# One-hots of a visit's destinations by one DVE comparison in attention and in messages of a graph network

## The chip, the cores and the metric

The kernel runs on one core of a Trainium2 chip as one program. The metric is the device time of that program in microseconds. The engines are TensorE (PE, with its weight loads as PEld), VectorE (DVE), ScalarE (ACT), GpSimd (POOL), and SyncE (SP), which here only starts transfers.

## The reference, cut to what matters

There are 3125 nodes with 64 features and 103125 edges, sorted by destination. Four layers follow each other, each on the normalized x and added to x: a propagation of ten hops, a three-layer graph convolution, attention over each node's incoming edges, and a message layer. The change touches the last two:

```python
# attention
qi = q[tgt]; e = edge_attr @ We; kj = k[src] + e; vj = v[src] + e
alpha = jnp.sum(qi * kj, axis=-1) / math.sqrt(C)         # two heads of 64
amax = jax.ops.segment_max(alpha, tgt, num_segments=n)
ex = jnp.exp(alpha - amax[tgt])
den = jax.ops.segment_sum(ex, tgt, num_segments=n)
agg = jax.ops.segment_sum((ex / (den[tgt] + 1e-08))[:, :, None] * vj, tgt, num_segments=n)
# messages
msg = jax.nn.relu(jnp.concatenate([edge_feat, hid[src]], axis=1) @ W1 + b1)
msg_sum = jax.ops.segment_sum(msg, dst, num_segments=N_NODES)
```

## The kernel before

The edges are cut into 403 tiles of 256, two halves of 128 edges on the partitions, and the nodes into blocks of 64 destinations. Since the edges are sorted, a tile meets one block or a few; a pair of a tile and a block that it may meet is a visit, and there are 451 visits (V2). The last 48 visits of a stage need no new tile. Which block and tile belong to a visit is found on the chip: each engine that needs the numbers loads them once in eight visits (`Blocks`) and addresses its operands through registers.

`stage_tables` makes, among others, `rel2`: for each edge of each visit its destination minus 64 times the block, in 32 bit floats. A value from 0 to 63 is a destination inside the block, anything else means that the edge belongs to another visit. Its steps on DVE are a chain: each waits for the one before. `iotaH` holds 0, 1, 2, ... in 16 bits on every partition.

`stage_attend` (from L1390 on). POOL gathers the source rows of each tile by two indirect DMAs of 128 rows (L1451), up to eight tiles ahead; SP brings edge features and the block's transformed queries (L1437, L1442). PE runs a loop with one step per visit: it transposes the next tile (L1465), scores a visit in one of two banks, transposes the exponentials of the visit two before (L1484) and sums the one three before (L1492). The score is the one-hot times `pen` (L1473) plus the query product (L1476). The one-hot of DVE holds 0 at an edge's destination and -1 elsewhere, in both heads' 64 columns, and `pen` is the unit matrix times 1e30, so that destinations that are not the edge's own get -1e30. DVE does for a visit: the maximum over a row (L1541), a one-hot half for the visit two ahead (L1531), the new running maximum (L1547), the other half (L1531), the difference (L1552), the accumulation of the visit three before (L1558) and the store of the maximum (L1561). ACT copies the transposed tile (L1503) and exponentials (L1508), and takes the two exponentials (L1513, L1514).

`stage_messages` (from L1800 on). Of each eight tiles, POOL gathers six from the message table (L1870), and DVE adds the gathered rows to the product of the edge features (L1902) in a bank (L2000). For the other two PE looks the rows up itself: DVE makes 25 comparisons of 512 edges with a chunk of the table (L2006), PE multiplies each with the table (L1909). ACT applies relu (L1945 from memory, L1942 from the bank). The one-hot of a visit is made by ACT in three instructions, max(0, 1 - |rel2 - iota|): twice the absolute value (L1951) and once the rest (L1957). PE sums the visit by the one-hot two steps later (L1918, four banks), and DVE accumulates (L2012). The one-hots are 32 bit floats there, in four buffers.

`stage_build` already makes its one-hots by paired comparisons (L447 to L449), with both operands read as pairs of 16 bit numbers.

Of the kernel before, what the change touches and what calls it, by code (L numbers as in the profile page):

```python
# [7 lines left out]
F32 = mybir.dt.float32  # L8
F16 = mybir.dt.float16
# [3 lines left out]
ALU = mybir.AluOpType  # L13
ACT = mybir.ActivationFunctionType
# [3 lines left out]
P = 128  # L18
# [11 lines left out]
T1 = -(-EDGES // TE)  # L30
# [26 lines left out]
BD = 64  # L57
# [3 lines left out]
V2 = T1 + J2 - 1  # L61
V2P = 460
# [40 lines left out]
class Mem:  # L103


    def __init__(self, nc, ctx):
        sb = lambda name, shape, dt: ctx.enter_context(nc.sbuf_tensor(name, shape, dt))
# [6 lines left out]
        self.work2 = sb("work2", [P, NDST + NCH * D], F32)  # L114
        self.rel2 = sb("rel2", [P, 2, V2P], F32)
        self.src2 = sb("src2", [P, 2, V2P], I32)
# [12 lines left out]
        sem = lambda n: ctx.enter_context(nc.semaphore(n))  # L129
# [31 lines left out]
    def small(self, i):  # L161

        return self.smalls[:, i * D:(i + 1) * D]

    def zbuf(self, k):

        base = self.work[:, 0:NCH * D] if k == 0 else self.work2[:, 3 * DC:3 * DC + NCH * D]
        return base.bitcast(F16).rearrange("p (a s d) -> p a s d", a=NCH, s=2)
# [5 lines left out]
def stage_tables(nc, m, last0, last, dst, src, edges):  # L174
# [4 lines left out]
    with ExitStack() as ctx:  # L179
        sem = lambda n: ctx.enter_context(nc.semaphore(n))  # L180
# [3 lines left out]
        def take(n):  # L184
            at[0] += n
            return raw[:, at[0] - n:at[0]]
# [19 lines left out]
        jI = m.work2[:, 2 * V0P:3 * V0P].bitcast(I32)  # L206
        src2F = take(2 * V2P).rearrange("p (h v) -> p h v", h=2)
        wmax, wall = take(1), take(1)
# [10 lines left out]
        for arr in range(4):  # L219
            for k in range(0, K1, 4):  # L220
                n = min(4, K1 - k)
                groups.append(([f1[:, k + i, arr, :] for i in range(n)], tabT[:, arr, k * P:(k + n) * P]))
        for arr, to in enumerate((m.rel2, src2F)):
            for h in range(2):
                groups.append(([f2[:, k, arr, h * P:(h + 1) * P] for k in range(K2)], to[:, h, 0:V2P]))
# [66 lines left out]
        def _(dve):  # L292
            chain = m.dve_step.on(dve)
# [5 lines left out]
            for s in schemes:  # L299
# [4 lines left out]
                for c in range(s["C"]):  # L304
                    ins = dve.tensor_scalar(s["cmp"][:, c, :], iotaF[:, 0:s["VP"]], s["end"][:, c:c + 1], None, ALU.is_gt)
                ins.then_inc(s_cmp, 1)
            for c in range(C0):
                ins = dve.tensor_scalar(cmpJ[:, c, :], iotaF[:, 0:J0], schemes[0]["blkF"][:, c:c + 1], None, ALU.is_ge)
# [71 lines left out]
            j2 = schemes[1]["jv"][:, 1:V2P + 1]  # L380
            for h in range(2):
                chain(dve.scalar_tensor_tensor(m.rel2[:, h, :], j2, -float(BD), m.rel2[:, h, :], ALU.mult, ALU.add))
            chain(dve.tensor_copy(m.src2[:, :, :], src2F))
# [819 lines left out]
BIG = 1e30  # L1203
# [37 lines left out]
def wait(eng, sem, n):  # L1241

    if not isinstance(n, int) or n > 0:
        eng.wait_ge(sem, n)
# [145 lines left out]
def stage_attend(nc, m, keep, x_out, q_out, ea, x_t, q_t):  # L1390
# [4 lines left out]
    with ExitStack() as ctx:  # L1395
# [121 lines left out]
        def _(dve):  # L1517
            dve.memset(rows[:, :, :, ONE:ONE + 1], 1.0)
            dve.memset(nmax, LOW)
            dve.tensor_scalar(pen, m.ident[:, :], BIG, None, ALU.mult)  # L1520
            for hd in range(HEADS):
# [4 lines left out]

            def onehot(v, s):

                if s == 0:
                    wait(dve, scored, v - 3)  # L1530
                ins = dve.tensor_scalar(oh[v % 4][:, s, :], iota2, m.rel2[:, s, v:v + 1], -1.0, ALU.is_equal, ALU.add)  # L1531
                if s == 1:
                    ins.then_inc(oh_ready, 1)

            for i in range(-2, V2 + 3):
# [7 lines left out]
                if v < V2:  # L1543
                    onehot(v, 0)
                if inside:
                    dve.wait_ge(s_small, 3 * i + 1)
                    dve.tensor_tensor(nm[s3], nmj, rm[s3], ALU.min).then_inc(s_small, 1)  # L1547
                if v < V2:
                    onehot(v, 1)
                if inside:  # L1550
# [249 lines left out]
def stage_messages(nc, m, keep, w1, w_out, b_out, o_in, ef_t, src, g_t):  # L1800

    with ExitStack() as ctx:
# [11 lines left out]
        oh = [halves(take(2 * BD)) for _ in range(4)]  # L1814
        away = [halves(take(2 * BD)) for _ in range(2)]
        T = [halves(take(2 * D)) for _ in range(4)]
# [16 lines left out]
        oh_ready = sem("ms_oh")  # L1833
        away_ready = sem("ms_away")
        summed = sem("ms_A")
# [87 lines left out]
        def _(act):  # L1923
            act.wait_ge(init, 1)
            for i in range(-2, V2):
                t = i
# [10 lines left out]
                if 0 <= t < T1:  # L1937
# [8 lines left out]
                    ins.then_inc(m_ready, 1)  # L1946
                v = i + 1
                if 0 <= v < V2:
                    wait(act, oh_ready, v - 1)
                    for s in range(2):  # L1950
                        ins = nc.scalar.activation(away[v % 2][:, s, :], m.iotaH[:, 0:BD], ACT.Abs, bias=m.rel2[:, s, v:v + 1], scale=-1.0)  # L1951
                    ins.then_inc(away_ready, 1)
                v = i
                if 0 <= v < V2:
                    act.wait_ge(away_ready, v + 1)
                    wait(act, summed, v - 3)
                    nc.scalar.activation(oh[v % 4], away[v % 2], ACT.Relu, bias=1.0, scale=-1.0).then_inc(oh_ready, 1)  # L1957

        @block.vector
        def _(dve):  # L1960
# [13 lines left out]
            def split():  # L1974
# [13 lines left out]
                dve.tensor_tensor(table[:, :, 1, :], wide, table[:, :, 0, :], ALU.subtract).then_inc(s_max, 1)  # L1988

            for i in range(-1, V2 + 3):  # L1990
                if i == 3:
                    split()
                t = i
                if 0 <= t < T1 and not on_pe(t):
# [180 lines left out]
```

## Time and profile before

| what | value |
|---|---|
| median of 3 runs | 3705.48 us |
| lowest and highest | 3702.94, 3708.67 us |
| span of the profiled execution | 4103.0 us |
| profiled execution's own time | not listed beside the runs; its span stands for it |
| busy share PE, PEld, DVE, ACT, POOL | 77%, 48%, 48%, 39%, 40% |
| TensorE clock granted, mean | 0.832 |
| attention's visits | 1640 to 2995 us |
| messages' visits | 3064 to 4070 us |

The profiled execution is 397.5 us longer than the median of the runs without a profile. Its durations are those of single instructions, start to end; instructions of one engine overlap by some tens of nanoseconds, so starts are compared with starts where pace matters. Register instructions don't count as busy.

### The profile page before, as it was taken

The page shows a single profiled execution, that of the slowest core. Times are in us where ns is not written, and L with a number is a line of the kernel's source. Part 1 is how long each engine was busy: PE and PEld are TensorE (multiplying, and loading weights), DVE is VectorE, ACT ScalarE, POOL GpSimd, SP SyncE. Part 2 cuts the span into 40 slices and gives each one's busy share as a digit, 9 for nine tenths or more (in the row PEclk, how much of TensorE's full clock was granted, in tenths as well). Part 3 has the DMA queues.
Part 4 walks back from the last instruction along what each step waited for, and adds up shares of the span by engine and source line. Part 5 has one row for each costly group of instructions (what it writes and reads, how often), then busy time and mean ns, then how long its engine had stood idle before and what let it go on. Part 6 is the DMA issues. An engine that isn't in the chain of part 4 may idle for free. (4 is left out here: it accounts for less than half of the span.)

```text
span 4103.0 us, 80080 instructions
## 1 busy us (share of the span) xinstructions
PE 3139.2 (77%) x17480; PEld 1972.5 (48%) x17480; DVE 1986.4 (48%) x6935; ACT 1606.3 (39%) x4621; POOL 1627.3 (40%) x1766
## 2 busy tenths in 40 slices
PE   3788788879997797577777777777866778787877
PEld 2444444444443343455566656556643444444445
DVE  6656666556656115344444444444673444444442
ACT  1555555413322001233333333333453444444445
POOL 2000000024333001666666666666106666666660
PEclk7899898999998998687777777877977888888885
DMA  1111111125557995322222222222112222222220
GB/s 38 57 59 57 57 59 59 51 93 193 188 177 261 406 360 185 65 54 55 54 55 54 55 54 53 54 55 54 40 28 56 66 63 66 64 66 63 66 61 13
DMA packets 417722, 370.64 MB, mean 90 GB/s; under 512 B 175608, under 2 KB 342232, under 8 KB 417336
## 3 DMA queue, kind: packets, MB, share of 16 engines
q1 hardware_dynamic: 365912, 315.65, 23.8%
q0 software_dynamic: 46144, 48.98, 6.5%
q8 instruction: 198, 3.24, 0.3%
q10 hardware_dynamic: 5280, 1.23, 0.1%
q14 instruction: 188, 1.54, 0.1%
HBM read 279.65 MB, written 86.00 MB: 89 GB/s over the span
## 5 line engine op out<-in xcount | busy, mean ns | idle before, releaser
L1451 POOL DMA_INDIRECT big<-row_table,src x806 | 761.5, 945 | 487.3 <-issue 183.4
L1870 POOL DMA_INDIRECT big<-message_table,src x610 | 612.0, 1003 | 394.5 <-DVE big L2000 172.1
L1476 PE MATMUL banks<-big 97*128 x902 | 399.8, 534 | 148.6 <-issue 138.1
L1492 PE MATMUL banks<-big 128*128 x1804 | 349.0, 326 | 174.8 <-ACT big L1508 110.1
L486 PE MATMUL banks<-work 128*128 128x226 f16 x1197 | 350.3, 293 | 138.6 <-issue 131.0
L1492 PEld LDWEIGHTS banks<-big 128*128 128x128 f32 x1804 | 312.4, 244 | 202.5 <-issue 202.1
L1909 PE MATMUL banks<-big 128*128 128x512 f16 x1225 | 395.6, 441 | 4.4 <-DVE big L1988 4.4
L850 PE MATMUL banks<-big,work 128*128 128x512 f16 (+1 forms) x1750 | 352.1, 359 | 22.3 <-DVE work L984 17.4
L1541 DVE TENSOR_REDUCE big<-banks 128x1 f32<-128x256 f32 x451 | 189.4, 420 | 332.5 <-PE banks L1476 183.8
L1508 ACT COPY big<-banks 128x256 f32<-128x256 f32 x451 | 169.8, 377 | 439.5 <-remote 194.0
L1918 PEld LDWEIGHTS banks<-big 128*64 128x64 f32 x1804 | 173.8, 164 | 343.6 <-issue 343.0
L1918 PE MATMUL banks<-big 128*64 x1804 | 247.5, 268 | 116.5 <-issue 98.3
L487 PE MATMUL banks<-work 128*128 128x200 f16 x1197 | 335.6, 280 | 0.0
L488 PE MATMUL banks<-work 128*128 128x200 f16 x1197 | 326.9, 273 | 0.0
L429 POOL COPY work<-work 128x100 f16<-128x100 f16 x120 | 35.9, 300 | 666.9 <-DVE work L452 649.9
L1558 DVE SCALAR_TENSOR_TENSOR big<-big,banks 128x97 f32 x451 | 142.4, 316 | 325.0 <-remote 208.5
L486 PEld LDWEIGHTS banks<-work 128*128 128x128 f16 x1197 | 121.9, 102 | 363.1 <-issue 350.1
L512 ACT ACTIVATE work<-banks 128x800 f32<-128x800 f32 x196 | 164.3, 838 | 330.6 <-PE banks L488 330.6
L908 POOL TENSOR_TENSOR work<-work 128x400 f16<-128x400 f32 x196 | 180.1, 946 | 284.8 <-DVE work L977 244.2
L2006 DVE TENSOR_SCALAR big<-big 128x512 f16<-128x512 f16 x1225 | 281.6, 285 | 2.3
L2000 DVE TENSOR_TENSOR big<-banks,big 128x128 f32<-128x128 f32 x305 | 87.3, 286 | 399.8 <-remote 257.3
L1476 PEld LDWEIGHTS banks<-big 97*128 97x128 f32 x902 | 177.4, 244 | 198.9 <-issue 196.4
(338 smaller groups left out, 5835.8 us busy)
## 6 DMA issues: line engine op xcount, KB each, us to landing
big<-weights_halves SPq DMA_DIRECT2D x16, 6400.0 KB, 20.8
weights_dense<-work SPq DMA_DIRECT2D x196, 200.0 KB, 1.9
work<-weights_dense SPq DMA_DIRECT2D x196, 200.0 KB, 2.7
weights_halves<-work SPq DMA_DIRECT2D x98, 400.0 KB, 2.6
big<-q_table SPq DMA_DIRECT2D x451, 64.0 KB
big<-in_ef SPq DMA_DIRECT2D x403, 64.0 KB
big<-in_ea SPq DMA_DIRECT2D x403, 32.0 KB
big<-row_table,src POOLq DMA_INDIRECT x806
```

The source lines that it names most:

```text
L486: pe.matmul(to(CW, CW + CAW), rows[:, 0, t, :], cols[:, t, :], start=False, stop=True, skip_group_check=True)
L487: pe.matmul(to(0, CW), rows[:, 1, t, :], cols[:, t, 0:CW], start=False, stop=True, skip_group_check=True)
L488: pe.matmul(to(0, CW), rows[:, 2, t, :], cols[:, t, 0:CW], start=False, stop=True, skip_group_check=True).then_inc(vis_done, 1)
L850: ins = pe.matmul(m.PB[c % 4][:, 0:width(c)], z[k][:, a, :, :], counts[:, a, c * DC:c * DC + width(c)], start=(a == 0), stop=(a == NCH - 1))
L1451: po.indirect_dma_start(rows[:, t % RT, s, 0:D], None, x_t.rearrange("a p c -> (a p) c"), bass.IndirectOffsetOnAxis(ap=m.src2[:, s, t:t + ...
L1476: pe.matmul(psS[v % 2], qT[v % R][0:XW, :], XF[0:XW, bass.ds(slot, 1), :].rearrange("p t e -> p (t e)"), start=False, stop=True).then_inc( ...
L1492: ins = pe.matmul(psA[v % 2], PT[v % 2][:, s * P:(s + 1) * P], rows[:, bass.ds(slot, 1), s, :].rearrange("p t c -> p (t c)"), start=(s == ...
L1541: dve.tensor_reduce(rm[s3], psS[i % 2], op=ALU.max, axis=X, negate=True).then_inc(s_small, 1)
L1870: po.indirect_dma_start(G[n % R][:, s, :], None, g_t.rearrange("a p c -> (a p) c"), bass.IndirectOffsetOnAxis(ap=m.src2[:, s, t:t + 1], ax ...
L1909: pe.matmul(psH[q % 2], table[:, a, :, :].rearrange("p s d -> p (s d)"), hot[n % HOT], start=(a == 0), stop=(a == NCH - 1)).then_inc(hot_u ...
L1918: ins = pe.matmul(psA[v % 4], oh[v % 4][:, s, :], M[:, bass.ds(slot, 1), s, :].rearrange("p t c -> p (t c)"), start=(s == 0), stop=(s == 1))
L2006: dve.tensor_scalar(hot[n % HOT], key[q % 2], float(P * a - CENTER), None, ALU.is_equal).then_inc(hot_ready, 1)
```

## The change

`rel2` becomes a table of 16 bit floats in which every number stands twice. It is clamped to -1 to 64 first, since large differences would not be exact in 16 bits. In attention one DVE instruction compares both halves of the tile with `iota2`; it gives 1 where the destination is another one and 0 where it is the edge's own, and `pen` changes its sign. It stands where the first of the two stood. In messages the three ACT instructions, their buffers and their semaphore are gone, and one DVE comparison stands at the head of each step of DVE's loop.

```diff
-        self.rel2 = sb("rel2", [P, 2, V2P], F32)
+        self.rel2 = sb("rel2", [P, 2, V2P, 2], F16)
+    def places(self, v, n):
+        return self.rel2[:, :, v, :].unsqueeze(2).to_broadcast([P, 2, n // 2, 2])
...
-                chain(dve.scalar_tensor_tensor(m.rel2[:, h, :], j2, -float(BD), m.rel2[:, h, :], ALU.mult, ALU.add))
+                chain(dve.scalar_tensor_tensor(dst2F[:, h, :], j2, -float(BD), dst2F[:, h, :], ALU.mult, ALU.add))
+                chain(dve.tensor_scalar(dst2F[:, h, :], dst2F[:, h, :], -1.0, float(BD), ALU.max, ALU.min))
+                chain(dve.tensor_copy(m.rel2[:, h, :, :], dst2F[:, h, :].unsqueeze(2).to_broadcast([P, V2P, 2])))
...
-            dve.tensor_scalar(pen, m.ident[:, :], BIG, None, ALU.mult)
+            dve.tensor_scalar(pen, m.ident[:, :], -BIG, None, ALU.mult)
...
-            def onehot(v, s):
-                if s == 0:
-                    wait(dve, scored, v - 3)
-                ins = dve.tensor_scalar(oh[v % 4][:, s, :], iota2, m.rel2[:, s, v:v + 1], -1.0, ALU.is_equal, ALU.add)
-                if s == 1:
-                    ins.then_inc(oh_ready, 1)
+            both = iota2.rearrange("p (r u) -> p r u", u=2).unsqueeze(1).to_broadcast([P, 2, P // 2, 2])
+            def others(v):
+                wait(dve, scored, v - 3)
+                dve.tensor_tensor(oh[v % 4].rearrange("p s (r u) -> p s r u", u=2), both, m.places(v, P), ALU.not_equal).then_inc(oh_ready, 1)
...
                 if v < V2:
-                    onehot(v, 0)
+                    others(v)
                 if inside:
                     dve.wait_ge(s_small, 3 * i + 1)
                     dve.tensor_tensor(nm[s3], nmj, rm[s3], ALU.min).then_inc(s_small, 1)
-                if v < V2:
-                    onehot(v, 1)
...
-                v = i + 1
-                if 0 <= v < V2:
-                    wait(act, oh_ready, v - 1)
-                    for s in range(2):
-                        ins = nc.scalar.activation(away[v % 2][:, s, :], m.iotaH[:, 0:BD], ACT.Abs, bias=m.rel2[:, s, v:v + 1], scale=-1.0)
-                    ins.then_inc(away_ready, 1)
-                v = i
-                if 0 <= v < V2:
-                    act.wait_ge(away_ready, v + 1)
-                    wait(act, summed, v - 3)
-                    nc.scalar.activation(oh[v % 4], away[v % 2], ACT.Relu, bias=1.0, scale=-1.0).then_inc(oh_ready, 1)
...
+            here = m.iotaH[:, 0:BD].rearrange("p (r u) -> p r u", u=2).unsqueeze(1).to_broadcast([P, 2, BD // 2, 2])
             for i in range(-1, V2 + 3):
                 if i == 3:
                     split()
+                v = i
+                if 0 <= v < V2:
+                    wait(dve, summed, v - 3)
+                    dve.tensor_tensor(oh[v % 4].rearrange("p s (r u) -> p s r u", u=2), here, m.places(v, BD), ALU.is_equal).then_inc(oh_ready, 1)
```

## Rows read from the trace of the kernel before

**Rows 1.** Busy us by stretch: PE, PEld, DVE, ACT, POOL; clock, DMA share, GB/s

```profile
1640.00:2890.00 1250.00, 903.02 (x4730) 731.22 (x4726) 532.21 (x2763) 463.87 (x1576) 762.21 (x807) 0.77 0.27 55
2890.00:2995.00 105.00, 85.34 (x573) 68.91 (x573) 75.60 (x397) 53.87 (x179) 0.00 (x0) 0.98 0.12 34
3064.00:4007.00 943.00, 729.57 (x3775) 396.87 (x3776) 397.63 (x1930) 431.35 (x1675) 612.04 (x610) 0.82 0.28 64
4007.00:4070.00 63.00, 43.77 (x263) 31.60 (x262) 15.03 (x69) 48.16 (x179) 0.00 (x0) 0.58 0.01 3
```

**Rows 2.** The page: gathers, busy us, mean ns of one, idle before

```profile
L1451 POOL DMA_INDIRECT big<-row_table,src x806 | 761.5, 945 | 487.3 <-issue 183.4
L1870 POOL DMA_INDIRECT big<-message_table,src x610 | 612.0, 1003 | 394.5 <-DVE big L2000 172.1
```

**Rows 3.** Timeline of a stall: start us, us, [idle before <-releaser]

```profile
2398.15 0.95 POOL L1451 DMA_INDIRECT big<-row_table,src  x1 [0.30 <-issue]
...
2398.38 0.39 PE L1465 MATMUL banks<-ident,big 128*97 128x128 f32 x2
...
2400.50 0.32 DVE L1558 SCALAR_TENSOR_TENSOR big<-big,banks 128x97 f32 x1 [3.31 <-remote]
2400.67 0.94 POOL L1451 DMA_INDIRECT big<-row_table,src  x1 [1.57 <-remote]
```

**Rows 4.** Waits of the whole run: engine, line, releaser: us, times, longest

```profile
DVE big L2000 <- remote: 257.3, 63, 15.3
...
DVE big L1558 <- remote: 208.5, 122, 3.3
...
PE banks L1902 <- ACT big L1942: 35.2, 23, 2.6
...
PE banks L1473 <- DVE big L1531: 3.7, 8, 0.5
```

**Rows 5.** Groups by shape on DVE, whole run

```profile
L2012 DVE TENSOR_TENSOR big<-big,banks 64x65 f32 x451 | 94.5, 210 | 189.6 <-PE banks L1918 105.1 <-issue 41.2 <-remote 37.3
L2000 DVE TENSOR_TENSOR big<-banks,big 128x128 f32<-128x128 f32 x305 | 87.3, 286 | 399.8 <-remote 257.3 <-PE banks L1902 122.2 <-issue 19.3
...
L449 DVE TENSOR_TENSOR work<-iotaH,work 128x260 f16<-128x260 f16 x120 | 34.4, 287 | 0.0
...
L383 DVE CAST src<-big 128x920 int32<-128x920 f32 x1 | 0.6, 639 | 0.0
```

**Rows 6.** Timeline of DVE in one visit of attention

```profile
2394.53 0.41 DVE L1541 TENSOR_REDUCE big<-banks 128x1 f32<-128x256 f32 x1
2394.86 0.25 DVE L1531 TENSOR_SCALAR big<-big,rel 128x128 bf16<-128x128 f16 x1
2395.23 0.16 DVE L1547 TENSOR_TENSOR big<-big 128x1 f32<-128x1 f32 x1
...
2395.47 0.15 DVE L1552 TENSOR_TENSOR big<-big 128x1 f32<-128x1 f32 x1
```

**Rows 7.** Timeline of messages behind its last gather

```profile
4028.35 1.47 PE L1918 MATMUL banks<-big 128*64 x8 [0.16 <-issue]
...
4028.97 0.22 DVE L2012 TENSOR_TENSOR big<-big,banks 64x65 f32 x1 [0.36 <-DVE big L2012]
...
4030.30 0.59 ACT L1951 ACTIVATE big<-iotaH,rel 128x64 f32<-128x64 f16 x2
...
4030.86 0.69 PE L1918 MATMUL banks<-big 128*64 x4 [0.16 <-issue]
...
4031.14 0.58 ACT L1951 ACTIVATE big<-iotaH,rel 128x64 f32<-128x64 f16 x2
...
4033.86 0.69 PE L1918 MATMUL banks<-big 128*64 x4 [1.30 <-DVE big L2012]
```

**Rows 8.** Timeline of messages, table comparisons beside a gather

```profile
3605.97 0.69 DVE L2006 TENSOR_SCALAR big<-big 128x512 f16<-128x512 f16 x3
...
3606.41 1.20 POOL L1870 DMA_INDIRECT big<-message_table,src  x1 [0.30 <-issue]
```

More of the change, by code:

```diff
@@ L206, in stage_tables @@
         jI = m.work2[:, 2 * V0P:3 * V0P].bitcast(I32)
-        src2F = take(2 * V2P).rearrange("p (h v) -> p h v", h=2)
+        src2F, dst2F = (take(2 * V2P).rearrange("p (h v) -> p h v", h=2) for _ in range(2))
         wmax, wall = take(1), take(1)
@@ L222, in stage_tables @@
                 groups.append(([f1[:, k + i, arr, :] for i in range(n)], tabT[:, arr, k * P:(k + n) * P]))
-        for arr, to in enumerate((m.rel2, src2F)):
+        for arr, to in enumerate((dst2F, src2F)):
             for h in range(2):
@@ L1814, in stage_messages @@
         oh = [halves(take(2 * BD)) for _ in range(4)]
-        away = [halves(take(2 * BD)) for _ in range(2)]
         T = [halves(take(2 * D)) for _ in range(4)]
@@ L1833, in stage_messages @@
         oh_ready = sem("ms_oh")
-        away_ready = sem("ms_away")
         summed = sem("ms_A")
@@ L1924, in _ @@
             act.wait_ge(init, 1)
-            for i in range(-2, V2):
+            for i in range(-2, T1):
                 t = i
```

## The prediction

> **What bounds the kernel now.** I read the page first, for the shares: TensorE (PE) is busy 77% of the span, DVE 48%, ACT 39%, POOL 40%, and none of these says what a visit waits for. So I cut the span at the stages that the change touches [rows 1]. Attention takes 1640 to 2995 us, the last 105 us of it without any gather; messages takes 3064 to 4070, the last 63 us nearly all without. In the two stretches with gathers PE is busy 72% and 77%, DVE 43% and 42%, ACT 37% and 46%, POOL 61% and 65%. TensorE's granted clock is 0.77 and 0.82 there, a mixture of its two levels, 1.2 and 2.4 GHz. No engine is full, and the share of POOL hides something: a gather is busy 0.945 us [rows 2], but 0.30 us of issue stands before each even when nothing else does [rows 3]. So 806 gathers need 806 x 1.25 = 1007 us of the 1250 us, and in messages, where one takes 1.003 us, 610 x 1.308 = 798 us of the 943 us. The loops run 243 and 145 us over POOL's floor.
>
> What fills the difference? The waits answer with a releaser that the profile can't name: "remote" stands behind 209 us of waiting of the accumulation in attention (L1558) and 257 us of the add in messages (L2000) [rows 4]. The timeline of one such stall shows what it is: the K transposes start at 2398.38 and take 0.39 us, yet DVE and POOL, which wait for PE's work, both resume only at 2400.50 and 2400.67, after 3.31 and 1.57 us of idleness [rows 3]. All the news of PE is late at once. I found such stalls only where gathers run.
>
> The profiled execution spans 4103.0 us, and the median of the runs is 3705.5, which is 397.5 less. The excess over POOL's floor is 243 + 145 = 388 us. I take these for the same time: without the profiler the two loops run close to POOL's gather rate. That is an inference, not a reading, and the chances below allow for its being wrong. The sum is made as differences on the profiled execution and carried over in microseconds.
>
> **Part 1, the tables.** rel2 is now made by a sum into a scratch row, a clamp and a doubling copy, for each of two halves. The sum stays. The copy writes 920 elements a partition, 0.64 us by L383; the clamp has half as many, and I give it the same for an upper bound [rows 5]. This is a serial chain on DVE with nothing beside it: 2 x 2 x 0.64 = +2.6 us, and not below +1.3.
>
> **Part 2, attention.** For each of 451 visits two comparisons of 0.25 us (L1531) go [rows 6], and one of 128 x 256 elements, all 16 bit, comes. L449 is nearly this instruction (a paired comparison with iotaH, 260 elements): 287 ns [rows 5]. DVE's busy time falls by 451 x (0.50 - 0.287) = 96 us. Little of it lies on a path, and the order of starts shows why [rows 6]. The first comparison starts 0.33 us after the reduction, and the minimum L1547 starts 0.37 us after that, although the comparison took only 0.25: register instructions for the block's column stand between (they don't count as busy). A comparison of 0.287 fits into the same 0.37. The second comparison runs inside the wait from L1547 to L1552: 0.24 us apart, of which L1547 itself is 0.16. Taking it out can bring L1552 forward by 0.08 at most; since L1552 must still see L1547's semaphore, I take half, 0.04. PE scores with two banks, so the loop from score through exponential to score spans two visits, and a visit gets 0.02 of it. If this loop set every visit, that were 403 x 0.02 = 8 us in the stretch with gathers; since POOL's floor sets part of them I take 4, and for the 48 visits behind them 1. The ends: 0, and 451 x 0.08 = 36 us. The one-hot is also ready earlier, but PE's wait for it is 3.7 us in all [rows 4]. The pen only changes its sign, and PE's work not at all.
>
> **Part 3, messages.** ACT loses two instructions and one (L1951 twice, L1957) a visit; its pace with them, in the stretch without gathers, is 0.84 us a visit (4030.30 to 4031.14) [rows 7]. DVE gets one comparison of 128 x 128 elements with 16 bit inputs and a 32 bit result. The trace has none. From below: 210 ns, L2012 with 65 elements. From above: 286 ns, L2000, 128 elements in 32 bit [rows 5]. I take 286, the row with the same element count. That is 451 x 0.286 = 129 us more on DVE, which brings it from 398 of 943 us in the gather stretch to about 515, 55%. The new wait (for the sum of visit v-4) adds nothing: DVE has waited for the same sum one step earlier, to accumulate it. Behind the new instruction on DVE queue the add L2000 of the tile, which frees POOL's buffer (eight tiles deep) and PE's bank (two deep), then the table comparisons and the accumulation. PE needs the one-hot of visit v two steps later, so none of this is tight.
>
> In the gather stretch I cost all this at 0: the cover is POOL, 6 tiles of 8 gathered, 12 x 1.308 = 15.7 us for eight visits. DVE needs in the same eight visits, from start to start, 25 x 0.23 for the table comparisons (0.69 for three [rows 8]), 6 x 0.29 for the adds, 8 x 0.58 for the accumulations (0.22 and 0.36 before it [rows 7]) and 8 x 0.29 for the new one: 14.4 us. That is under 15.7, but not by much. If the cover is gone, the relief of ACT counts too: PE waits 35.2 us for L1942, ACT's exit of the bank [rows 4], which no longer stands behind one-hots.
>
> In the 48 visits behind the last tile ACT's pace is close to what is seen. PE takes 0.69 + 0.16 = 0.85 us a visit there, and 1.47/2 = 0.735 where two visits run together; every eighth visit waits 1.3 us more for DVE, which loads its next block numbers [rows 7]. Without ACT's pace I give PE 0.735 for each visit: 48 x 0.115 = 6 us less. The ends: 0, because DVE must then do 0.58 for the accumulation and part of 0.29 for the comparison (0.87 at worst, no better than now), and 12, if the wait of each eighth visit shrinks too.
>
> **The sum.** +2.6 - 4 - 1 - 6 = -8.4 us, so 3705.5 - 8.4 = 3697 us, 0.2% faster. What a measurement of this kernel can tell from no change is 0.2%, 7.4 us: the forecast lies on that border.
>
> **A rule to weigh.** In attention two one-hot comparisons fall beside many a gather, and the gathers take 945 ns on average, with 0.94 in the rows that I looked at [rows 2, 3]: at most 0.005 x 806 = 4 us hang on it. In messages a gather beside trains of table comparisons takes 1.20 us [rows 8], and the mean is 1.003. The Trainium skill, page "SBUF — State Buffer", section "Who interferes with whom", says that a tensor_scalar can take the port pair that DVE shares with GpSimd and then holds off descriptor writing, while a tensor_tensor with two SBUF inputs contends only with GpSimd's reads. By that rule the change helps attention's gathers and leaves those of messages alone. The trace agrees for the trains in messages and shows next to nothing of it in attention.
>
> **The rivals.**
> 1. The forecast, small gains at the ends of the two loops: 0.47; 3688 to 3706.
> 2. The loops are not at POOL's floor without the profiler, and latency counts. Then attention's 451 x 0.04 = 18, the 6 of messages' end and 0 to 35 for PE's wait on L1942 come off, and the tables' 2.6 come on: 3684 to 3649, at half the wait 3667. For it: PE also waits in the gather-free stretches. Against it: 388 against 397. Chance 0.18.
> 3. Nothing moves: DVE's comparison takes the place of ACT's pace at the end of messages, and attention hides all: 3705.5 + 2.6 = 3708. Chance 0.14.
> 4. Slower: the new comparison slows POOL's gathers, which are the floor. The trains cost (1003 - 945) x 610 = 35 us over 1225 table comparisons, 0.029 us each; 451 more at this price are 13 us, at twice the price, as they lengthen a train, 26. Without gains and with the tables that gives 3721 to 3734; if each held a gather up for its full 0.286 wherever one runs (65% of the time), 84 us. It decides from 0.035 us for each, where it has eaten the 8.4 us and added 7.4. Against it: attention's L1547 and L1552, which have two inputs in SBUF too, though of one column, run beside its gathers, and these take 945 ns. Chance 0.13.
> 5. Slower: DVE's 14.4 us for eight visits is too low and passes POOL's 15.7, and the adds come late. At 1.5 to 1.8 us more for eight visits it costs 49 x 0.2 to 0.5 = 10 to 25 us: 3715 to 3730. Chance 0.08.
>
> **How the numbers follow.** Case 1 gives 0.26 to faster and 0.21 to no change, case 2 goes to faster, 3 to no change, 4 and 5 to slower: 0.44, 0.35, 0.21. The range runs from the middle of case 2, rounded to 3670, into case 4, 3722, and leaves out about half of either.
>
> **What would show it.** Right: in attention L1547's counterpart still starts 0.37 us after the comparison, L1552's about 0.20 after L1547's; a visit of messages behind the last tile takes about 0.9 us, waits for block numbers included, and not 0.85 + 1.3/8 = 1.01; gathers keep 945 and 1003 ns; PE no longer waits for L1942. Wrong: gathers in messages above 1.03 us (case 4); the new comparisons far from 0.29 us; DVE above 60% in messages with PE waiting for L2000 (case 5); or loops that get shorter by tens of microseconds with POOL's times unchanged, which would say that POOL's floor was not the bound.

## The result and the profile after

The changed kernel takes 3750.97 us (median of 4 runs, 3747.97 to 3754.76), the kernel before 3706.15 us (4 runs, 3702.94 to 3708.67). The ratio is 1.0117, with a 95% interval from 1.0104 to 1.0131: 44.8 us or 1.2% slower. The forecast was 3697 us with a range up to 3722; sign and range are both wrong.

The page of the changed kernel, busy shares and the two gathers:

```profile
span 3752.9 us, 78285 instructions
...
PE 2949.0 (79%) x17480; PEld 1839.4 (49%) x17480; DVE 2101.8 (56%) x6939; ACT 1319.1 (35%) x3268; POOL 1669.7 (44%) x1766
...
L1457 POOL DMA_INDIRECT big<-row_table,src x806 | 764.1, 948 | 249.7 <-issue 228.8
L1871 POOL DMA_INDIRECT big<-message_table,src x610 | 651.5, 1068 | 251.4 <-issue 177.8
```

Attention's gathers keep their length (945 ns before, [rows 2]). Those of messages go from 1003 to 1068 ns: 610 gathers, 651.5 us busy and not 612.0. Of the 251.4 us of idle time in front of them 177.8 is issue, and 65.7 stands before the first one, so in the loop POOL waits for next to nothing.

Busy time by stretch of the changed kernel: attention with gathers and behind them, messages with gathers and behind them (us, then PE, PEld, DVE, ACT, POOL, granted clock, DMA share, GB/s).

```profile
1650.00:2666.00 1016.00, 799.98 (x4804) 641.63 (x4800) 537.85 (x2411) 484.76 (x1605) 765.87 (x807) 0.90 0.33 69
2666.00:2760.00 94.00, 77.58 (x516) 62.31 (x516) 65.74 (x302) 46.65 (x152) 0.00 (x0) 0.98 0.12 32
2829.00:3667.00 838.00, 659.22 (x3836) 364.97 (x3837) 509.98 (x2347) 178.73 (x500) 651.52 (x610) 0.93 0.30 72
3667.00:3720.00 53.00, 34.71 (x202) 25.45 (x202) 21.54 (x103) 0.31 (x1) 0.00 (x0) 0.50 0.01 2
```

These can't be set against [rows 1] directly: the span is 350 us shorter than the 4103.0 us of the first profile of the kernel before, although the kernel is slower. So the first experiment was the kernel before once more.

### The profile page after: what moved, and what is told of

It reads as the page before. It is cut to its first block and busy times, and to the rows that moved or that the text cites. A ratio compares the mean times of both kernels' runs of the same rounds, so it can differ in the third digit from the quotient of the medians.

```text
span 3752.9 us, 78285 instructions
## 1 busy us (share of the span) xinstructions
PE 2949.0 (79%) x17480; PEld 1839.4 (49%) x17480; DVE 2101.8 (56%) x6939; ACT 1319.1 (35%) x3268; POOL 1669.7 (44%) x1766
## 5 line engine op out<-in xcount | busy, mean ns | idle before, releaser
L1871 POOL DMA_INDIRECT big<-message_table,src x610 | 651.5, 1068 | 251.4 <-issue 177.8
L1482 PE MATMUL banks<-big 97*128 x902 | 347.5, 471 | 88.7 <-issue 84.4
L1910 PE MATMUL banks<-big 128*128 128x512 f16 x1225 | 349.7, 398 | 4.7 <-DVE big L1977 4.7
L1946 ACT ACTIVATE big<-big 128x128 f32<-128x128 f32 x305 | 94.9, 311 | 644.7 <-DVE big L1994 631.2
L2000 DVE TENSOR_SCALAR big<-big 128x512 f16<-128x512 f16 x1225 | 308.6, 306 | 0.0
L1498 PE MATMUL banks<-big 128*128 x1804 | 289.6, 287 | 0.0
L1919 PE MATMUL banks<-big 128*64 x1804 | 225.1, 253 | 56.7 <-issue 39.8
L1471 PE MATMUL banks<-ident,big 128*97 128x128 f32 x806 | 189.2, 320 | 102.3 <-DMA big<-row_table,src 90.7
L1065 PE MATMUL banks<-big,work 128*128 128x512 f16 x900 | 217.7, 406 | 60.8 <-DMA big<-weights_halves 51.2
L1498 PEld LDWEIGHTS banks<-big 128*128 128x128 f32 x1804 | 264.2, 211 | 0.4 <-issue 0.3
```

Source lines behind the costliest of these rows:

```text
L1065: pe.matmul(out, z[l % 2][:, a, :, :], st[buffer(l, c)][:, 0:n // BP, s, a * BP:(a + 1) * BP], start=(a == 0 and s == 0), stop=False)
L1482: pe.matmul(psS[v % 2], qT[v % R][0:XW, :], XF[0:XW, bass.ds(slot, 1), :].rearrange("p t e -> p (t e)"), start=False, stop=True).then_inc( ...
L1498: ins = pe.matmul(psA[v % 2], PT[v % 2][:, s * P:(s + 1) * P], rows[:, bass.ds(slot, 1), s, :].rearrange("p t c -> p (t c)"), start=(s == ...
L1871: po.indirect_dma_start(G[n % R][:, s, :], None, g_t.rearrange("a p c -> (a p) c"), bass.IndirectOffsetOnAxis(ap=m.src2[:, s, t:t + 1], ax ...
L1910: pe.matmul(psH[q % 2], table[:, a, :, :].rearrange("p s d -> p (s d)"), hot[n % HOT], start=(a == 0), stop=(a == NCH - 1)).then_inc(hot_u ...
L1919: ins = pe.matmul(psA[v % 4], oh[v % 4][:, s, :], M[:, bass.ds(slot, 1), s, :].rearrange("p t c -> p (t c)"), start=(s == 0), stop=(s == 1))
```

## The experiments

Each ratio is against the kernel before on the same chip, in the same series of runs.

**The kernel before once more** (no edit).

> The kernel before, unchanged, for a second profile. Theory A (the kernel runs at POOL's gather rate, and the stalls of the first profile belonged to that execution): a span near 3705 us, attention's gathers start every 1.25 us in the mean, messages' gathers every 1.30 to 1.31 us (mean duration 1.00 us), against 1.373 (1.068 us) in the kernel after; about 38 us of the difference of 45 us lie there. Theory B (latency of ACT and DVE bounds the loops, and POOL only seems to): POOL waits for other engines in both loops as in the first profile, and the mean distance of gathers is clearly above 1.31 us in messages.

It took 3707.0 us with a span of 3705.2 us. Its page and its stretch of messages with gathers:

```profile
L1451 POOL DMA_INDIRECT big<-row_table,src x806 | 761.8, 945 | 248.9 <-issue 226.5
L1870 POOL DMA_INDIRECT big<-message_table,src x610 | 610.1, 1000 | 250.6 <-issue 177.1
```

```profile
2822.00:3618.00 796.00, 638.78 (x3830) 357.21 (x3830) 433.58 (x1944) 439.15 (x1706) 610.05 (x610) 0.95 0.31 76
3618.00:3673.00 55.00, 36.36 (x209) 26.30 (x208) 12.49 (x56) 40.43 (x149) 0.00 (x0) 0.50 0.01 2
```

A profile without stalls exists: neither loop has a wait for "remote" in it (the two of the whole run, 4.1 us, belong to the stages ahead), and its span with 1.8 us around it is the run's own time. The loops run at POOL's rate: from the first to the last gather start, attention takes 1006.3 us (1.250 a gather), messages 794.8 us (1.305), the 1007 and 798 us that the prediction had worked out.

With this trace the account of one profiled execution of each kernel can be made. The starts of the first and the last gather of each loop in the changed kernel:

```profile
1655.80 1.19 POOL L1457 DMA_INDIRECT big<-row_table,src  x1 [4.08 <-POOLq L1264]
...
2664.58 0.95 POOL L1457 DMA_INDIRECT big<-row_table,src  x1 [0.30 <-issue]
...
2829.09 0.96 POOL L1871 DMA_INDIRECT big<-message_table,src  x1 [65.72 <-POOLq L1570]
...
3665.39 0.95 POOL L1871 DMA_INDIRECT big<-message_table,src  x1 [0.31 <-issue]
```

| stretch | before | changed | difference |
|---|---|---|---|
| start to first gather of attention | 1650.1 | 1655.8 | +5.7 |
| attention's gathers | 1006.3 | 1008.8 | +2.5 |
| last one to messages' first gather | 165.8 | 164.5 | -1.3 |
| messages' gathers | 794.8 | 836.3 | +41.5 |
| last gather to the end of the span | 88.3 | 87.5 | -0.8 |

The sum, 47.6 us, is the difference of the spans (47.7). Of the +5.7 the tables are 2.2; the rest is what single executions differ by in the stages ahead, which the change doesn't touch: an execution of the changed kernel further down has its first gather at 1648.3 us and 1006.5 us of attention's gathers. Only the +41.5 stands out of this.

**Each half of the change alone.** The rival theories were now: A, the comparison in messages lengthens the gathers; C, the tables and attention have a part in it. Attention alone (the doubled numbers are copied at the stage's start from `rel2`, which stays a table of 32 bit floats; messages as before):

```diff
-                ins = dve.tensor_scalar(oh[v % 4][:, s, :], iota2, m.rel2[:, s, v:v + 1], -1.0, ALU.is_equal, ALU.add)
+                dve.tensor_tensor(oh[v % 4]..., both, rel16[:, :, v, :]..., ALU.not_equal).then_inc(oh_ready, 1)
```

> Only attention gets the single paired comparison; its 16 bit pairs are copied from the unchanged 32 bit rel2 when the stage begins (about 2 us), and messages keeps ACT's three instructions. Theory A (POOL's gathers set attention, and nearly all of the loss is in messages, where the change of that stage alone gave 1.010): ratio 1.000 to 1.002, attention's gathers every 1.25 us, messages' every 1.305. Rival C (attention lost too, by a comparison with two inputs in SBUF beside the gathers): 1.003 or more, most of it in longer gathers.

Measured: 3705.5 us against 3709.5, ratio 0.9994 [0.9985, 1.0004]; gathers 946 and 1003 ns, attention's first to last start 1006.7 us. Attention's half does nothing that can be told from the scatter.

Messages alone (attention as before, the same copy at the head of messages):

```diff
-                        ins = nc.scalar.activation(away[v % 2][:, s, :], m.iotaH[:, 0:BD], ACT.Abs, ...)
-                    nc.scalar.activation(oh[v % 4], away[v % 2], ACT.Relu, ...)
+                    dve.tensor_tensor(oh[v % 4]..., here, rel16[:, :, v, :]..., ALU.is_equal).then_inc(oh_ready, 1)
```

> Only messages gets DVE's comparison, from pairs copied when the stage begins; attention keeps two comparisons. Theory A (the whole loss is that messages' gathers take longer beside a DVE that has no pause left): ratio 1.011 to 1.013, gathers of messages 1.06 to 1.08 us in the mean. Rival C (the loss is spread over both stages or sits in the tables): 1.004 to 1.008.

Measured: 3743.2 us, ratio 1.0102 [1.0084, 1.0120]; gathers 945 and 1067 ns. The loss is this half; the ratio is just under the expected 1.011 to 1.013, the gathers are inside the expected length.

**Is it the instruction on DVE, or that ACT no longer makes the one-hots?** Two kernels keep ACT's one-hots and add to DVE, where the comparison would stand, an instruction whose result nobody reads (both also make the copy at the head of messages). The expectations speak of two theories: P, that an instruction of DVE holds a gather up by its second input in SBUF; D, that any further instruction does it, because it closes DVE's pauses. The first kernel adds the comparison itself.

```diff
+                    dve.tensor_tensor(nowhere[v % 2]..., here, rel16[:, :, v, :]..., ALU.is_equal).then_inc(idle_done, 1)
```

> The kernel before, ACT's one-hots kept, plus the comparison of the kernel after at the same place, its result thrown away. Both theories P and D: gathers of messages 1.36 to 1.38 us apart, ratio 1.010 to 1.012. A rival E, that the kernel after lost by taking the one-hots from ACT (their order or their time of arrival) and not by DVE's instruction, expects 1.000 here.

Measured: 3741.4 us, ratio 1.0093 [1.0076, 1.0110]; gathers of messages 1061 ns, 1.366 us apart. What was taken from ACT has next to no part in the loss, and saves nothing.

The second is a reduction over 128 numbers of `iotaH`, with one input and one number a partition as output.

```diff
+                    dve.tensor_reduce(nowhere[v % 2][:, 0, 0:1], m.iotaH[:, 0:P], op=ALU.max, axis=X).then_inc(idle_done, 1)
```

> The kernel before, ACT's one-hots kept, plus one reduction of 128 columns of iotaH to one column on DVE at the head of each visit of messages (0.25 to 0.3 us, one input, result thrown away). Theory P (a gather is held up by DVE instructions that use a second SBUF port or input): the reduction doesn't count, messages' gathers stay at 1.305 us apart and the ratio at 1.000 to 1.001. Theory D (any further instruction on DVE closes the pauses in which a gather gets through): gathers at 1.36 to 1.38 us apart, ratio 1.010.

Measured: 3738.9 us, ratio 1.0083 [1.0067, 1.0100]; gathers of messages 1052 ns, 1.357 us apart: a little under what theory D expected, and far from theory P. So neither the second input nor the size of the output makes up most of the cost; the same 0.27 us on DVE costs nearly the same.

**The comparison with its iota in PSUM.** Bank 5 holds the iota as 32 bit floats, so only three banks are left for the sums.

```diff
-        psA = [m.PB[2 + i][0:BD, 0:MW] for i in range(4)]
+        psA = [m.PB[2 + i][0:BD, 0:MW] for i in range(3)]
+            dve.tensor_copy(m.PB[5][:, 0:BD], m.iotaH[:, 0:BD])
-            here = m.iotaH[:, 0:BD]...
+            here = m.PB[5][:, 0:BD]...
```

> The kernel after, with messages' comparison reading iota from a PSUM bank of its own as 32 bit numbers, so that it has one input in SBUF; the sums get three banks instead of four. The comparison should take about 0.29 us as now. Theory P: gathers of messages return to 1.30 us apart or less, and the ratio to the kernel before is 0.998 to 1.002. Theory D: nothing changes, 1.011 to 1.013.

Measured: 3726.7 us, ratio 1.0046 [1.0029, 1.0063]; gathers of messages 1019 ns. The instruction is no shorter (0.27 us), and the loss is less than half. Both expectations missed: P expected no loss, D all of it.

Now one gather in each of four traces, beside the same work of DVE: the turn of eight tiles in which PE looks up two tiles itself, so that DVE has no landing to wait for and runs without a stop. In the changed kernel the lines of messages on DVE are others: L2000 is the table comparison (L2006 before), L2006 the accumulation (L2012 before), L1994 the add (L2000 before), L1986 the new comparison. First the kernel before (start us, us, engine, line):

```profile
3299.05 0.68 DVE L2006 TENSOR_SCALAR big<-big 128x512 f16<-128x512 f16 x3
...
3299.19 1.46 POOL L1870 DMA_INDIRECT big<-message_table,src  x1 [0.30 <-issue]
...
3299.65 0.20 DVE L2012 TENSOR_TENSOR big<-big,banks 64x65 f32 x1
3299.78 0.68 DVE L2006 TENSOR_SCALAR big<-big 128x512 f16<-128x512 f16 x3
...
3300.39 0.20 DVE L2012 TENSOR_TENSOR big<-big,banks 64x65 f32 x1
3300.90 0.29 DVE L2000 TENSOR_TENSOR big<-banks,big 128x128 f32<-128x128 f32 x1 [0.31 <-PE banks L1902]
3300.95 0.94 POOL L1870 DMA_INDIRECT big<-message_table,src  x1 [0.30 <-issue]
```

The changed kernel:

```profile
2984.68 1.80 POOL L1871 DMA_INDIRECT big<-message_table,src  x1 [0.30 <-issue]
2984.74 0.68 DVE L2000 TENSOR_SCALAR big<-big 128x512 f16<-128x512 f16 x3
...
2985.35 0.20 DVE L2006 TENSOR_TENSOR big<-big,banks 64x65 f32 x1
2985.48 0.28 DVE L1986 TENSOR_TENSOR big<-iotaH,rel 128x128 f32<-128x128 f16 x1
...
2985.68 0.68 DVE L2000 TENSOR_SCALAR big<-big 128x512 f16<-128x512 f16 x3
...
2986.29 0.20 DVE L2006 TENSOR_TENSOR big<-big,banks 64x65 f32 x1
...
2986.79 1.77 POOL L1871 DMA_INDIRECT big<-message_table,src  x1 [0.30 <-issue]
...
2986.82 0.27 DVE L2000 TENSOR_SCALAR big<-big 128x512 f16<-128x512 f16 x1
```

The kernel before with the reduction added:

```profile
3037.61 1.78 POOL L1874 DMA_INDIRECT big<-message_table,src  x1 [0.30 <-issue]
...
3038.40 0.27 DVE L2003 TENSOR_REDUCE work<-iotaH 128x1 f32<-128x128 f16 x1
...
3039.20 0.20 DVE L2023 TENSOR_TENSOR big<-big,banks 64x65 f32 x1
```

And the changed kernel with the iota in PSUM:

```profile
3010.20 1.59 POOL L1871 DMA_INDIRECT big<-message_table,src  x1 [0.31 <-issue]
...
3010.99 0.27 DVE L1987 TENSOR_TENSOR big<-banks,rel 128x128 f32<-128x128 f32 x1
3011.19 0.69 DVE L2001 TENSOR_SCALAR big<-big 128x512 f16<-128x512 f16 x3
...
3011.80 0.20 DVE L2007 TENSOR_TENSOR big<-big,banks 64x65 f32 x1
```

A gather alone takes 0.94 us. The four that are set side by side here (1.46, 1.80, 1.78 and 1.59 us) start beside a train of three table comparisons and don't end until the train behind it ends, or nearly so. In the kernel before, the gather ends at 3300.65, 0.26 us after the second accumulation starts; from one accumulation to the next are 0.74 us. In the changed kernel that distance is 0.94 us, because the comparison stands in it, and the gather ends at 2986.48, 0.19 us after the second accumulation starts. With the reduction it is 3039.39, again 0.19 us after. With the iota in PSUM the distance is 0.94 us too, but the gather ends at 3011.79, ahead of the second accumulation: as if it had got something done during the comparison. Counted over the traces, 43 gathers of messages last over 1.3 us before and 79 after. Of these, 40 and all 79 run beside a stretch of at least 2 us in which DVE has no pause over 0.06 us. (Most gathers beside such a stretch are not long: 145 run beside one before, 185 after.)

The next gather matters as much. Before, it starts just behind a pause of DVE of 0.31 us, and takes 0.94 us; in the changed kernel it starts at 2986.79 with DVE still in its train (the view ends at 2987; the comparison at 2986.82 is the first of four), and takes 1.77. Of the 79 long gathers 26 stand right behind another long one; of the 43 none does. The gathers can be sorted by the step of DVE in which they start (a step goes here from one accumulation's start to the next). About 45 start in the step of the first of the two tiles without a gather, about 60 in the step behind the second:

| mean length of gathers, ns | in the step of the first tile without a gather | in the step behind the second |
|---|---|---|
| before | 1445 | 958 |
| changed | 1747 | 1308 |
| before + comparison thrown away | 1716 | 1202 |
| before + reduction | 1600 | 1227 |
| changed, iota in PSUM | 1530 | 1071 |

Of the 41.5 us, 12.8 arise in the one step and 19.9 in the other (13.1 and 23.1 in the trace of the changed kernel further down). So nearly half of the loss is not the first long gather but a second one behind it, and with the input in PSUM both are shorter.

**Does the loss go with the trains?** The 25 table comparisons of the two looked-up tiles are dealt out evenly over eight steps (three each, and four in the last), the three steps in which DVE catches up among them. A new deal gives nothing to the steps of the two tiles without a gather, two to the step behind them, and five or four to the others:

```diff
-    return [(q, a) for q, t in enumerate(chains()) for u in range(GP) if i == t - 5 + u for a in range(u * NCH // GP, (u + 1) * NCH // GP)]
+    share = (0, 5, 10, 15, 19, 23, 23, 23, 25)
+    return [(q, a) for q, t in enumerate(chains()) for u in range(GP) if i == t - 5 + u for a in range(share[u], share[u + 1])]
```

It went on both kernels, together with the reduction from PSUM on the kernel before (three banks for the sums, like above; theory F: an input in PSUM leaves a gather room) and two combinations: attention's half with the new deal, and the iota in PSUM with the new deal. All eight runs of these came to a chip on which the kernel before takes 4140.8 us (4136.2 in the second series).

> As the dummy reduction of iotaH (ratio 1.0083, messages' gathers 1.357 us apart), but it reads its 128 columns from a PSUM bank, with three banks for the sums. Theory F (an instruction of DVE whose large input lies in PSUM leaves a gather room, one whose inputs lie in SBUF does not, whatever its kind): gathers 1.31 to 1.33 us apart, ratio 1.001 to 1.005. Theory D (every further instruction of DVE counts alike, and the kernel with iota in PSUM was better for another reason, as ACT's relief): gathers 1.35 to 1.36 us apart, ratio 1.007 to 1.009.

> The kernel after, with the 25 table comparisons of eight steps dealt out anew: none in DVE's two steps of the tiles that need no gather, where 43 of 44 gathers of the kernel after took over 1.2 us (1.75 us in the mean), and five or four in the others. Theory T (gathers are held up where DVE catches up and trains of comparisons follow each other with one short pause between): messages' gathers 1.25 to 1.30 us apart, 45 to 75 us less than the kernel after, ratio to the kernel before 0.992 to 1.000. Theory N (every comparison costs a gather the same, wherever it stands): 1.37 us apart, 1.011 to 1.013.

> The kernel before with the same new shares. Theory T: gathers of messages from 1.305 to 1.26 to 1.29 us apart, ratio 0.991 to 0.998. Theory N: 1.305 us apart, ratio 1.000.

> Attention's single comparison and the new shares, messages' one-hots on ACT. Attention is at its gathers' rate in either form, so this should equal the kernel before with the new shares within 0.1%: theory T 0.990 to 0.998, theory N 1.000.

> The kernel after with iota in PSUM and the new shares of table comparisons. On a chip where the kernel before takes about 3707 us: theories F and T together, gathers 1.25 to 1.28 us apart and a ratio of 0.990 to 0.997, the lowest of the four; if F is wrong, as the kernel after with new shares alone.

| kernel on the slower chip | ratio to before |
|---|---|
| before, reduction from PSUM added | 1.0042 [1.0027, 1.0056]; again 1.0052 [1.0034, 1.0070] |
| changed, new deal | 1.0061 [1.0045, 1.0078]; again 1.0086 [1.0068, 1.0104] |
| before, new deal | 1.0037 [1.0023, 1.0051]; again 1.0056 [1.0038, 1.0074] |
| attention's half, new deal | 1.0037 [1.0025, 1.0050] |
| changed, iota in PSUM, new deal | 1.0083 [1.0065, 1.0101] |

The expectations above have a chip of 3707 us in mind: the ratios of the kernels with the new deal lie outside them, and the reduction's 1.0042 lies where theory F had it, but not for theory F's reason, as the gathers are not what bounds the loop here. These traces look like the first profile: the page and the waits of the kernel with the reduction from PSUM show

```profile
L1874 POOL DMA_INDIRECT big<-message_table,src x610 | 626.2, 1026 | 408.3 <-DVE big L2012 185.3
```

```profile
DVE big L2012 <- remote: 248.7, 57, 11.6
...
DVE big L1558 <- remote: 202.2, 115, 3.5
```

POOL is idle for 408 us in messages there, not 251, and waits for DVE's adds (L2012 is the add in that kernel). The gathers are not the floor, and a gather's length doesn't carry through: with the reduction from PSUM the mean is 1026 ns and the first and last start 968.3 us apart, in the kernel before with the new deal 1002 ns and 969.5 us. So the question could not be answered. What these runs do answer is another: such stalls need no profiler, since the other executions on this chip take as long as the profiled one. They come with the chip, or with its state in these two series.

**The same kernels on a chip of 3707 us.** First the changed kernel unchanged, for the scatter, and with the new deal.

> The kernel after, unchanged, on the chip of this call. If the kernel before takes about 3707 us here: 1.010 to 1.013 again. If it takes about 4140 us: POOL waits for PE in both loops there, so longer gathers have some cover; theory A expects a smaller loss than 45 us, ratio 1.002 to 1.009. A rival, that the loss never was POOL's floor but DVE's own time, expects the same 1.012 or more.

> The kernel after with the new shares. If the kernel before takes about 3707 us here: theory T 0.992 to 1.000 with gathers 1.25 to 1.30 us apart, theory N 1.011 to 1.013. If it takes about 4140 us: 1.006 to 1.009 as in the two calls before; if the unchanged kernel after is below that, the new shares themselves cost time there.

Measured: the changed kernel 3749.0 us, 1.0110 [1.0093, 1.0127], gathers of messages 1072 ns. With the new deal 3714.6 us against 3707.3, ratio 1.0017 [1.0007, 1.0026] over 10 runs, gathers 1006 ns and 1.311 us apart, both just outside theory T's range and far from theory N's:

```profile
L1872 POOL DMA_INDIRECT big<-message_table,src x610 | 613.5, 1006 | 250.2 <-issue 174.9
```

The same 451 comparisons and 1225 table comparisons, only dealt otherwise, and 34 of the 42 us are gone. Gathers over 1.3 us: 18, and none of them in the steps of the two tiles without a gather; those that start in the first of these take 1034 ns on average, and not 1747.

> The kernel before plus the dummy reduction reading PSUM. If the kernel before takes about 3707 us here: theory F (a large input in PSUM leaves a gather room) gathers of messages 1.31 to 1.33 us apart, ratio 1.001 to 1.005; theory D (every further instruction counts alike) 1.35 to 1.36 us apart, ratio 1.007 to 1.009. If it takes about 4140 us: 1.004 to 1.005 again, and F stays open.

> The kernel before with the new shares of table comparisons. If the kernel before takes about 3707 us here: by what the shares gave the kernel after (34 us of its 41), 0.993 to 0.999 with gathers 1.26 to 1.30 us apart. A rival G, that a train of five costs a lone gather what it saves elsewhere, expects 0.999 to 1.003. If it takes about 4140 us: 1.004 to 1.006 again.

Measured: the reduction from PSUM 3720.9 us against 3702.6, 1.0046 [1.0030, 1.0063], gathers 1021 ns, where the one from SBUF gave 1.0083 and 1052. The kernel before with the new deal 3688.9 us, ratio 0.9957 [0.9941, 0.9974], gathers 975 ns: faster than both kernels. On the slower chip the same edit costs 0.4 to 0.6%.

| on the chips of 3703 to 3710 us | messages' gathers, ns | first to last start, us | ratio |
|---|---|---|---|
| before | 1000 | 794.8 | 1 |
| changed | 1068 | 836.3 | 1.0117 |
| before + comparison thrown away | 1061 | 832.1 | 1.0093 |
| before + reduction | 1052 | 826.3 | 1.0083 |
| before + reduction from PSUM | 1021 | 807.5 | 1.0046 |
| changed, iota in PSUM | 1019 | 806.3 | 1.0046 |
| changed, new deal | 1006 | 798.2 | 1.0017 |
| before, new deal | 975 | 779.6 | 0.9957 |

In each row the distance of the starts grows by what 610 gathers grow in length (68 ns x 610 = 41.5 us in the second row), which is what a floor does.

## Why the prediction was wrong, point by point

**The floor** was right: without the stalls the two loops run at 1.250 and 1.305 us a gather. The cause given for the 397.5 us was not: runs without the profiler take 4140 us too on one chip, so the first profile, whose chip isn't on record, was most likely taken on such a one. The equality of 388 and 397 us, which the prediction offered as evidence, fits both, and that the floor came out right in spite of it is luck in part.

**The step that failed is part 3, "in the gather stretch I cost all this at 0: the cover is POOL".** It compared DVE's time with POOL's as if POOL's were fixed. But the cover was the gathers, and the gathers are what a DVE instruction lengthens. The term put at 0 measured +41.5 us, 0.092 us for each of the 451 comparisons.

**Rival 4 named this mechanism and mis-sized it.** Its price was 0.029 us, from (1003 - 945) x 610 spread over 1225 table comparisons, and its upper estimate twice that, 26 us; the full length was worked out, 84 us, but left outside the range. The mean was the mistake: the table comparisons don't cost 0.029 each. With the new deal all 1225 are still made and the gathers take 975 ns, so a part of them costs nothing and a part costs much, those in the steps where DVE catches up. A new instruction in every step also stands in those steps, and there it lengthens the stretch that a gather has to outlast by its 0.20 us from start to start, and makes DVE's run long enough that the next gather starts in it too. [rows 8], with one gather of 1.20 us beside one train, showed a single gather's price; the trace of the kernel before also has 29 gathers over 1.3 us, 25 of them beside a stretch of DVE of at least 2 us without a pause over 0.06 us, and a look for the longest would have shown it.

**Against the rival** stood that attention's small two-input instructions run beside gathers of 945 ns. They still do, and so does the new comparison of 256 elements there, with 948 ns (945 and 946 in two other traces that have it): an instruction of DVE between pauses costs the gathers nothing. That told nothing of trains.

**The rule of the Trainium skill** (page "SBUF — State Buffer", section "Who interferes with whom") would have left the gathers of messages alone, since a tensor_tensor with two SBUF inputs contends only with GpSimd's reads; the same section says that a tensor_reduce never contends on trn2. The runs differ on both: +61 ns a gather with the comparison added, +52 with the reduction, though 21 of these 52 come with an input in PSUM as well (with one bank less for the sums). The measurement decides. The other half of the rule, that attention's gathers gain when 902 tensor_scalars go, isn't seen either: 945 and 946 ns.

**The tables**, +2.6: measured +2.2. The DVE timeline of the changed kernel:

```profile
79.92 0.40 DVE L387 TENSOR_SCALAR big<-big 128x460 f32<-128x460 f32 x1
80.36 0.64 DVE L388 CAST rel<-big 128x920 f16<-128x920 f32 x1
81.03 0.64 DVE L386 SCALAR_TENSOR_TENSOR big<-big 128x460 f32<-128x460 f32 x1
```

A clamp and a copy take 1.11 us from start to start (79.92 to 81.03), twice that is 2.2; the bound taken for the clamp, 0.64, was 0.40.

**Attention**, -5: measured about 0. The ratio of its half alone, 0.9994 [0.9985, 1.0004], leaves room for a few us, but its gathers' first and last start are 1006.7 us apart, and 1006.3 before. DVE in one visit of the changed kernel, to be read against [rows 6]:

```profile
2000.36 0.28 DVE L1538 TENSOR_TENSOR big<-big,rel 128x256 bf16<-128x256 f16 x1
2000.74 0.16 DVE L1552 TENSOR_TENSOR big<-big 128x1 f32<-128x1 f32 x1
2000.93 0.16 DVE L1555 TENSOR_TENSOR big<-big 128x1 f32<-128x1 f32 x1
```

The minimum starts 0.38 us after the comparison (forecast 0.37) and the difference 0.19 after the minimum (forecast 0.20, before 0.24), so the edit did what was said. It is worth nothing in the stretch with gathers because POOL sets the pace there.

**The end of messages**, -6: measured -0.8. PE of the changed kernel, behind the last gather:

```profile
3691.71 0.69 PE L1919 MATMUL banks<-big 128*64 x4 [1.26 <-DVE big L1986]
...
3692.56 0.69 PE L1919 MATMUL banks<-big 128*64 x4 [0.16 <-issue]
...
3693.42 0.69 PE L1919 MATMUL banks<-big 128*64 x4 [0.17 <-issue]
```

This is [rows 7] again, 0.85 us a visit and 1.3 at every eighth, with no one-hots on ACT. So ACT's 0.84 us a visit was not what set it. The clock is 0.50, the lower level, in both.

**Rival 5** had DVE's need too high. From the same timelines a table comparison takes 0.20 us from start to start, an add 0.20, an accumulation 0.13 and a new comparison 0.20: 25 x 0.20 + 6 x 0.20 + 8 x 0.33 = 8.8 us for eight visits, not 14.4. The 0.58 for an accumulation came from the stretch without gathers, where DVE waits for PE. Of the signs that the prediction named, case 4's came, gathers above 1.03 us. But case 5's came too: DVE is busy for 61% of messages' stretch with gathers (510.0 of 838 us), and PE waits more for the add (L1902, L2000 before and L1903, L1994 after). The waits of the whole run, before and then changed:

```profile
PE banks L1902 <- DVE big L2000: 27.0, 47, 1.8
POOL big L1870 <- DVE big L2000: 8.5, 28, 0.3
```

```profile
PE banks L1903 <- DVE big L1994: 69.5, 93, 3.1
POOL big L1871 <- DVE big L1994: 7.9, 26, 0.3
```

What tells the two cases apart is POOL: by case 5 its gathers would wait for late adds, and they wait 7.9 us in all, no more than before, while their own length accounts for the whole +41.5. PE's wait for L1942, 20.5 us before (at L1918), is gone as forecast.

**Open.** Why an input from PSUM leaves the gather room is not shown, only that the long gathers are shorter with it; the two kernels that show it also have three banks for the sums instead of four, which was not tried by itself. Their gathers account for 11.5 and 12.7 us of 17 and 18, and behind the last gather both take 90.2 us, not 88.3. How DVE and a gather get in each other's way isn't shown either: the runs show when, not by what. The unchanged new kernel was not run on the slower chip, and what makes the stalls there is not known.

## What to carry to other kernels

When another engine's work is the cover for an added instruction, ask first whether the instruction lengthens that work; a cover that is itself the bound gives no cover. Don't spread a contention over all the instructions that may cause it: sort the bound operation by its length, look at what surrounds the longest, and ask whether the new instruction falls there. And moving work into the pauses may be worth more than taking it away: dealing the table comparisons out of DVE's catch-up steps won 0.4% where gathers set the pace, and lost 0.4 to 0.6% on the chip where they did not. Where an added instruction makes one bound operation long, look at the next one too: it may start where it didn't before.

## What the runs showed of the hardware

- A gather of 128 rows takes 0.94 us beside single DVE instructions and up to 2.17 us in the changed kernel beside stretches of DVE of 2 us and more without a pause over 0.06 us; all 79 over 1.3 us lie there. The kind of the instruction that is added to these stretches matters little: with a comparison with two inputs the mean is 1061 ns, with a reduction with one 1052 ns. With the reduction's input in PSUM (and one bank less for the sums) it is 1021 ns.
- The same kernel took 3703 to 3710 us on four chips and 4136 to 4141 us on a fifth, with a granted clock of 0.90 and 0.83 over the run. In the first profile (4103.0 us) the two loops with gathers take 1244.6 and 941.0 us and not 1006.3 and 794.8, which is 384 of the 398 us, and there all news of PE comes late at once; an edit can have opposite signs on the two (0.9957 and 1.0037).
- DVE's instructions of 0.27 to 0.31 us follow each other at 0.20 us from start to start in a train, and an accumulation is followed after 0.13 us.
